# Softplus of the step widths shared out between ScalarE and GpSimd in chunks 2 to 4 of a fused state-space and expert kernel

## What is computed

```python
u = silu(causal_conv(x @ in_proj_x))
dt, B, C = split(u @ x_proj.T)                     # 64, 16 and 16 columns
delta = softplus(dt @ dt_proj.T + dt_b)            # 256 channels
h_t = exp(delta * A) * h_(t-1) + delta * B * u     # 256 channels x 16 states
y = (h * C).sum(states) + u * D
x1 = layernorm(x + (y * silu(res)) @ out_proj.T)
```

## Time and profile before

| | us |
|---|---|
| median of 3 runs | 480.37 (479.71 to 483.02) |
| the profiled execution's own time | 480.05 |
| its span, first to last instruction | 478.3 |

### The profile page before, as it was taken

One profiled execution on the slowest core, in us unless ns is written; L12 is line 12 of the kernel. 1 busy time (PEld: TensorE's weight loads), 2 busy tenths in 40 slices (PEclk: granted clock), 3 DMA queues, 4 the chain that ended last, 5 costly groups with the idle time before them and its releaser, 6 DMA issues.

```text
span 478.3 us, 6017 instructions
## 1 busy us (share of the span) xinstructions
PE 407.7 (85%) x1680; PEld 246.4 (52%) x1680; DVE 408.9 (85%) x890; ACT 319.4 (67%) x521; POOL 230.5 (48%) x203
## 2 busy tenths in 40 slices
PE   4989777679268999999967799999496999999993
PEld 3333222243124777755423478766132687778873
DVE  4569999999999999999999889999989765675654
ACT  3887246458544999999963778874746579587231
POOL 0049599899574475456964724656962000000000
PEclk9989989999597999999997599999789899999997
DMA  8496398998245455556853723575750000000000
GB/s 288 168 332 223 110 302 292 320 311 277 86 176 187 166 175 177 181 161 194 275 185 105 248 88 120 165 229 158 251 200 2 0 1 0 3 0 23 1 1 22
DMA packets 22065, 74.19 MB, mean 155 GB/s; under 512 B 2320, under 2 KB 4368, under 8 KB 21648
## 3 DMA queue, kind: packets, MB, share of 16 engines
q1 hardware_dynamic: 22032, 73.82, 46.7%
HBM read 72.50 MB, written 1.31 MB: 154 GB/s over the span
## 4 chain that ended last, share of the span: by engine, by line
PE 50%; DVE 26%; issue 11%; ACT 7%; POOL 4%; DMA 2%; SPq 1%; DVEq 0%; ACTq 0%; POOLq 0%
PE ps_g L719 11%; PE ps_y L626 10%; PE ps_u L764 10%; DVE ps_state L1127 7%; PE ps_u L719 6%; DVE product L1144 4%; PE ps_state L719 2%; DMA hidden<-w_up 2%; DVE drive L1127 2%; POOL drive L999 2%; DVE delta L1111 2%; DVE delta L1113 2%; PE ps_y L764 1%; POOL product L1020 1%; DVE stats L1154 1%
## 5 line engine op out<-in xcount | busy, mean ns | idle before, releaser
L999 POOL TENSOR_TENSOR drive<-du,b_row 128x512 f32<-128x512 f32 x128 | 164.9, 1308 | 51.0 <-DVE ps_state L1127 37.3
L626 PE MATMUL ps_y<-product,par 128*128 128x512 f32 x256 | 135.6, 648 | 21.1 <-DVE product L1144 12.7
L865 ACT ACTIVATE ps_state<-delta,decay_rate 128x512 f32<-128x512 f32 x128 | 85.5, 688 | 58.3 <-DVE product L1144 45.2
L626 PEld LDWEIGHTS ps_y<-product,par 128*128 128x128 f32 x256 | 47.9, 204 | 81.8 <-issue 32.7
L782 ACT ACT_TABLE_LOAD x69 | 88.5, 1283 | 1.9 <-PEq L1385 0.7
L1020 POOL TENSOR_TENSOR product<-drive,c_row 128x512 f32<-128x512 f32 x38 | 48.4, 1274 | 55.3 <-DVE drive L1127 51.3
L1144 DVE TENSOR_TENSOR product<-ps_state,c_row 128x512 f32<-128x512 f32 x90 | 60.2, 679 | 1.3 <-PE ps_y L626 1.0
L764 PEld LDWEIGHTS ps_u<-wd,hidden 128*128 128x128 f32 x448 | 53.8, 192 | 4.9 <-issue 2.0
L1127 DVE TENSOR_TENSOR_SCAN ps_state<-ps_state,carry,drive 128x512 f32<-128x512 f32 x44 | 55.3, 1274 | 0.3 <-ACT ps_state L865 0.3
L1127 DVE TENSOR_TENSOR_SCAN ps_state<-ps_state,drive 128x512 f32<-128x512 f32 x46 | 54.6, 1213 | 0.9 <-ACT ps_state L865 0.8
L764 PE MATMUL ps_u<-wd,hidden 128*128 128x128 f32 x448 | 54.9, 276 | 0.0
(11 more groups left out here) (253 smaller groups left out, 600.5 us busy)
## 6 DMA issues: line engine op xcount, KB each, us to landing
b_row<-bc_dram SPq DMA_DIRECT2D x64, 512.0 KB, 5.0
c_row<-bc_dram SPq DMA_DIRECT2D x64, 512.0 KB, 4.1
x_in<-x_t SPq DMA_DIRECT2D x4, 256.0 KB, 6.9
gelu<-w_gate SPq DMA_DIRECT2D x1, 1024.0 KB, 9.1
hidden<-w_up SPq DMA_DIRECT2D x1, 1024.0 KB, 10.9
wd<-w_down SPq DMA_DIRECT2D x1, 1024.0 KB, 12.8
...
```

What stands on the lines that cost most here:

```text
L626: mm(ps_y[:, :], ident, product[:, g % PRODUCTS, :], start=False, stop=(n == STATE - 1)).then_inc(y_pe, 1)
L865: nc.scalar.activation(ps_state[g % RING][:, :], delta[:, c % 2, h, :], ACT.Exp, scale=decay_rate[:, h, n:n + 1]).then_inc(decay_act, 1)
L999: nc.gpsimd.tensor_tensor(drive[:, g % DRIVES, :], du[:, h, :], b_row[:, m % ROWS, n % 2, :], ALU.mult).then_inc(drive_pool, 1)
```

## The change

1. ScalarE makes 1 + e (into `delta`) and that less 1 (in place, with a new constant tile `minus_one`), between `sp_exp` and `sp_ln`, in all four chunks: 2 instructions for each half.
2. In chunks 1 to 3, GpSimd makes the three others (`settle`): e less that, plus `sp_relu`, plus `sp_ln`. In chunk 0 they stay with VectorE. The waits of the ring of two `delta` buffers move to ScalarE, and ScalarE's second half now waits for GpSimd's first instruction of the first half.
3. `PLACES` is new for all engines.

```diff
@@ scalar, pre @@
                     if h:
-                        after(act, pre_dve, c, "a0")
+                        rest_made(act, c, 0)
                         after(act, pre_act, c, "ln0")
                     do(pre_act, sp_exp[:, :], sp_abs[:, h, :], ACT.Exp, scale=-1.0)
                     after(act, pre_act, c, f"exp{h}")
+                    if c >= 2:
+                        act.wait_ge(decay_act, UNITS * (c - 1))
+                        act.wait_ge(du_pool, HALVES * (c - 1))
+                    do(pre_act, delta[:, q, h, :], sp_exp[:, :], ACT.Identity, bias=1.0)
+                    after(act, pre_act, c, f"one{h}")
+                    do(pre_act, delta[:, q, h, :], delta[:, q, h, :], ACT.Identity, bias=minus_one[:, :])
                     do(pre_act, sp_ln[:, h, :], sp_exp[:, :], ACT.Ln, bias=1.0)
@@ gpsimd @@
+            def settle(c, h):
+                q = c % 2
+                if c == 0:
+                    return
+                after(pool, pre_act, c, f"less{h}")
+                nc.gpsimd.tensor_tensor(delta[:, q, h, :], sp_exp[:, :], delta[:, q, h, :],
+                                        ALU.subtract).then_inc(delta_pool.sem, 1)
+                after(pool, delta_pool, c - 1, f"rest{h}")
+                after(pool, pre_act, c, f"relu{h}")
+                nc.gpsimd.tensor_tensor(delta[:, q, h, :], sp_relu[:, h, :], delta[:, q, h, :],
+                                        ALU.add).then_inc(delta_pool.sem, 1)
+                after(pool, delta_pool, c - 1, f"b{h}")
+                after(pool, pre_act, c, f"ln{h}")
+                nc.gpsimd.tensor_tensor(delta[:, q, h, :], delta[:, q, h, :], sp_ln[:, h, :],
+                                        ALU.add).then_inc(delta_pool.sem, 1)
@@ vector, make_delta @@
-                after(dve, pre_act, c, f"exp{h}")
-                do(pre_dve, v.tensor_scalar(delta[:, q, h, :], sp_exp[:, :], 1.0, -1.0, ALU.add, ALU.add))
-                own(pre_dve, c, f"t{h}")
-                do(pre_dve, v.tensor_tensor(delta[:, q, h, :], sp_exp[:, :], delta[:, q, h, :], ALU.subtract))
+                if c:
+                    return
+                after(dve, pre_act, c, f"less{h}")
+                do(first_dve, v.tensor_tensor(delta[:, q, h, :], sp_exp[:, :], delta[:, q, h, :], ALU.subtract))
@@ PLACES, gpsimd @@
+        "settle 1": (6.069, 6.7586),
+        "settle 2": (0.9655, 1.1034),
+        "settle 3": (0, 0.5517),
```

More of the change, by code:

```diff
@@ L250, in build @@
         eps = sb("eps", [P, 2])
+        minus_one = sb("minus_one", [P, 1])
         side_g = sb("side_g", [P, SIDE])
@@ L430, in after, with rest_made, delta_made @@
             eng.wait_ge(marks.sem, marks.done(c, name))
+        def rest_made(eng, c, h):
+            if c == 0:
+                after(eng, first_dve, 0, f"rest{h}")
+            else:
+                after(eng, delta_pool, c - 1, f"rest{h}")
+        def delta_made(eng, c, h):
+            if c == 0:
+                after(eng, first_dve, 0, f"delta{h}")
+            else:
+                after(eng, delta_pool, c - 1, f"delta{h}")
         def tokens(c):
@@ L793, in setup @@
                 act.wait_ge(loaded_first, 16)
-                act.wait_ge(pool_const, 3)
+                act.wait_ge(pool_const, 4)
                 do(setup_act, decay_rate[:, :, :], par_of("a_log").rearrange("p (h n) -> p h n", h=HALVES), ACT.Exp)
@@ L853, in step @@
                 if n == 0:
-                    after(act, pre_dve, c, f"delta{h}")
+                    delta_made(act, c, h)
                 if g == 0:
@@ L977, in _ @@
             nc.gpsimd.memset(eps[:, 1:2], RMS_EPS).then_inc(pool_const, 1)
+            nc.gpsimd.memset(minus_one[:, :], -1.0).then_inc(pool_const, 1)
+            def settle(c, h):
+                q = c % 2
+                if c == 0:
+                    return
[10 more added lines that the diff above has]
+                                        ALU.add).then_inc(delta_pool.sem, 1)
             def make_du(c, h):
-                after(pool, pre_dve, c, f"delta{h}")
+                delta_made(pool, c, h)
                 if c:
@@ L1033, in pair @@
                                         product[:, g % PRODUCTS, :], ALU.add).then_inc(pair_pool, 1)
-            run("gpsimd", du=make_du, step=step, multiply=multiply, pair=pair, tail=tail)
+            run("gpsimd", settle=settle, du=make_du, step=step, multiply=multiply, pair=pair, tail=tail)
         @block.vector
@@ L1103, in make_delta @@
                 q = c % 2
-                if c >= 2:
-                    dve.wait_ge(decay_act, UNITS * (c - 1))
-                    dve.wait_ge(du_pool, HALVES * (c - 1))
-                after(dve, pre_act, c, f"exp{h}")
-                do(pre_dve, v.tensor_scalar(delta[:, q, h, :], sp_exp[:, :], 1.0, -1.0, ALU.add, ALU.add))
-                own(pre_dve, c, f"t{h}")
-                do(pre_dve, v.tensor_tensor(delta[:, q, h, :], sp_exp[:, :], delta[:, q, h, :], ALU.subtract))
-                own(pre_dve, c, f"a{h}")
-                do(pre_dve, v.tensor_tensor(delta[:, q, h, :], delta[:, q, h, :], sp_relu[:, h, :], ALU.add))
-                own(pre_dve, c, f"b{h}")
+                if c:
+                    return
+                after(dve, pre_act, c, f"less{h}")
+                do(first_dve, v.tensor_tensor(delta[:, q, h, :], sp_exp[:, :], delta[:, q, h, :], ALU.subtract))
+                own(first_dve, c, f"rest{h}")
+                do(first_dve, v.tensor_tensor(delta[:, q, h, :], sp_relu[:, h, :], delta[:, q, h, :], ALU.add))
+                own(first_dve, c, f"b{h}")
                 after(dve, pre_act, c, f"ln{h}")
-                do(pre_dve, v.tensor_tensor(delta[:, q, h, :], delta[:, q, h, :], sp_ln[:, h, :], ALU.add))
+                do(first_dve, v.tensor_tensor(delta[:, q, h, :], delta[:, q, h, :], sp_ln[:, h, :], ALU.add))
             def step(c, k):
```

9 lines of the change are left out of this document (5 added, 4 removed), and 193 rows, old and new, of the table PLACES.

## The result

The changed kernel takes 481.97 us (median of 20 runs, 480.00 to 484.02), the kernel before 480.32 (20 runs, 473.96 to 483.09). The ratio is **1.0066, 95% interval 1.0041 to 1.0091**: slower, where the prediction had 474.5 us. It lies inside what I had called "within 1%", but clear of noise on the other side of no change. The profiled execution took 482.71 us. The kernel before, compared with itself in experiment 10, gave 0.9974 (0.9922 to 1.0026), so differences of half a per cent between two experiments are not read.

What follows compares the result with a forecast made beforehand. VectorE was taken to bound S0, T1 and T2, TensorE F0, F1 and END. Terms -3.6 - 2.6 + 8.2 - 2.6 - 4.3 - 0.5 = -5.4 us on 480.05 gave 474.7, taken as 474.5; range 464 to 483.

Steps and rivals of the forecast that it cites:

- within 1%: Whole kernel: outcome no more than 1% from the kernel before, up to 485.2 us; chance 0.38.
- S0: First scan to chunk 0's logits: 4.6 us shorter, from 3.6 gained at the logits and a start 1.0 later.
- With them gone VectorE has fewer instructions that can be held up.: L1111 to L1116, 0.69 us alone and 1.65 beside GpSimd, leave VectorE, so fewer of its instructions can be held up.
- From gating to x1, 9.0 us.: Tail of chunk 0: 9.0 us from gating to x1 as before, so x1 starts at 107.0.
- T1, +8.2.: Stretch T1: nine more scans, six products and one gating, less 7.5 us of `delta`, make it 8.2 us longer.
- In S0 VectorE works 120.7 of 123.0 us ... so an instruction taken from VectorE counts.: VectorE is busy nearly throughout S0, T1 and T2, so instructions taken from it count there; 15.6 us lie in S0.
- Start, +1.0.: Start of chunk 0: two ScalarE instructions replace one of VectorE per half; first scan 1.0 us later, at 36.5.
- Chunk 0 up to the gating.: GpSimd's list sets the pace; VectorE waits 4 us for the 16th drive, gating at 98.0 in place of 101.55.
- under 52 us: Sign for T1: if it is not longer than 52 us, the count of scans is not what sets it.
- `settle` at 1.27 us.: GpSimd's 18 new instructions in chunks 1 to 3 take 1.27 us each, 22.9 us together, up to 29.7.
- F0 -2.6, F1 -2.6, T2 -4.3, END -0.5.: Later stretches shorten: three `finish` fewer in F0 and F1 each, three scans and a product in T2, one `finish` and scan in END.
- GpSimd becomes the bound: Rival, around the 16th drive and chunk 2's `settle`: S0's gain becomes a loss, T1 still pays; 481 to 486, chance 0.13.

Runs made afterwards that it cites:

- experiment 10: Kernel before and changed kernel each run once more, unaltered; ratios to the kernel before 0.9974 and 1.0067.
- experiment 2: Kernel before's softplus code in the changed kernel's new order, deltas of chunks 1 to 3 placed anew on VectorE; ratio to the kernel before 1.0226.
- experiment 1: Changed kernel's code with every engine in the old order, only `settle` placed anew; ratio to the kernel before 1.0097.
- experiment 3: Changed kernel with `settle` on one column in place of 512, all waits kept; ratio to the kernel before 0.9927.
- experiments 5 and 6: Changed kernel with GpSimd waiting until `shift` is done, ahead of drive 39 or ahead of drive 41; ratios to the kernel before 1.0000 and 0.9978.
- second pair of profiles: Profiles of the kernel before and the changed kernel, each run again unaltered; T1 48.0 and 64.1 us.
- e6: Changed kernel with GpSimd waiting for `shift` ahead of drive 39, and for the second softplus of chunks 0 and 1; ratio to the kernel before 1.0078.
- experiment 11: Kernel before with VectorE's four softplus instructions of chunks 1 to 3 cut to one column; ratio to the kernel before 0.9855.

## Why the prediction was wrong

The profiled execution was to become 5.4 us shorter and became 2.6 longer. By the terms of the sum the 8 us are: start 2.4, S0 3.7, F0 0.6, T1 4.1, F1 -2.2, T2 0.3, END -0.9.

- **"With them gone VectorE has fewer instructions that can be held up."** This step failed: the sum has no term for instructions that are held longer than before. Outside `delta` 11 us were held before and 22 after, 5 us more in S0 and 5 more in T1, with no more instructions on VectorE. The new order alone raises the sum to 19 (experiment 2; `shift` 6.3 to 12.4 us), the sharing alone to 18 (experiment 1), and the length of `settle` has no part in it (experiment 3).
- **From gating to x1, 9.0 us.** This is where it struck in S0: 12.5 us (100.84 to 113.30), 3.5 too many of the 3.7 that S0 is off, as `shift` was held for 4.71. The gaps of experiments 5 and 6 show it. From x1 to L1218 8.7 us were predicted and 8.7 measured, with 3.8 us of idle VectorE (4). With the gap for `shift` S0 is 119.3, 3.6 below before, where the prediction had 4.6.
- **T1, +8.2.** Right in what it counts: nine scans (11.1 us), products and gating 4.6 for 4.8, `delta` 7.5 less. Measured +12.3, and +16 between the second pair of profiles. What it lacks is held time outside `delta`, 7.3 us where it was 2.2 (the four of the second softplus 6.4 us in place of 2.5, and single instructions on 128x4), 10.7 in the second profile; VectorE is busy 58.9 us of T1, 62.1 in the second profile, 46.2 before. Here the cause is read from these sums only: when a gap took 2.7 us of it away (e6), T1 did not get shorter. My bound for what would refute the term (under 52 us) was on the wrong side.
- **"In S0 VectorE works 120.7 of 123.0 us ... so an instruction taken from VectorE counts."** In S0 it does: 7.0 us less of busy time gave 6 (experiment 11). But 5.7 of the 15.6 us on `delta` in chunks 1 and 2 were not work: six instructions were held 0.95 us above their shortest form.
- **Start, +1.0.** +3.4 in the profiled execution, of which 2.4 are matmuls that ran longer in this execution; without them +0.4 to 0.9.
- **Chunk 0 up to the gating.** Right within 1 us: the six `settle` stand from 59.3 to 68.5 us, the gating comes 61.9 us behind the first scan, against 66.0 before (61.5 predicted). The wait ahead of the 16th scan is 2.7 us and not 4; 68.6 less 8.7 plus 3 is 62.9, and not the 62 that the prediction took, so its own terms gave 3.
- **`settle` at 1.27 us.** Right. Its cost in S0, which the prediction had as the wait at the 16th drive, is 4.4 us by experiment 3, 3.3 of them waits for drives.
- **F0 -2.6, F1 -2.6, T2 -4.3, END -0.5.** Measured -2.0, -4.8 (second pair -3.4), -4.0 (-2.0) and -1.4 (-1.7): right in kind. F1's gain of 2.2 more than forecast was not looked into, and is luck as far as the total goes.
- **The rivals.** Nearest was "GpSimd becomes the bound", 481 to 486 with 0.13. Its place and its price (1.65 us for each `settle`) were wrong, but its core, that S0 gains almost nothing while T1 pays in full, is what came. The Trainium skill, GPSIMD Engine Reference, "Key points", names the shared SBUF interfaces. I had used it for two-input instructions of 128x512 alone; here instructions of 128x4 and 128x1 were held as well.

What stays open: why `shift` is held over four of GpSimd's instructions, when most others are let in at the end of one (0.95 us above their form), `shift` itself among them in the kernel before (1.25 us, to 110.50, with GpSimd's next instruction from 110.44 on and no pause between). The Trainium skill, SBUF — State Buffer, "Who interferes with whom", says that the ports which the two engines share are an exclusive lock: whoever issues first has them for the whole instruction, and the other is blocked. The rows of 1.64 and of 1.21 us agree; the 4.71 us, over four instructions, go beyond it. Open too is how much of the order's 11 us in experiment 2 is my placing.
